# A decoder layer on one core: scans and three fillers in the routing of the experts, and a last norm without waits on stores

## The reference

```python
x = _layernorm(x + _L0_attn_ref(x, Wq, Wkv, q_g, q_b, k_g, k_b, Wwin, bwin, Wout))
x = _layernorm(x + _L0_xattn_ref(x, ctx_1024, ctx_1024))
x = _layernorm(x + _L0_ffn_ref(x, router_w, expert_w1, expert_w2))
# _L0_ffn_ref:
scores = xf @ router_w.T
top_v, top_i = jax.lax.top_k(scores, TOP_K)
routing_w = jax.nn.softmax(top_v, axis=-1)
for e in range(NUM_EXPERTS):
    w_e = jnp.sum(jnp.where(top_i == e, routing_w, 0.0), axis=-1)
    h = jax.nn.gelu(xf @ expert_w1[e].T, approximate=False)
    out = out + h @ expert_w2[e].T * w_e[:, None]
```

## Time and profile before

| | us |
|---|---|
| median of 3 runs | 1164.17 (1163.9 to 1164.26) |
| the profiled execution | 1166.83 |
| its span | 1164.9 |
| from the last `attend` to the first fetch of rows | 643 to 687.7 |
| the experts | 688 to 1129.4 |
| the last norm | 1129.4 to 1164.9 |

### The profile page before, as it was taken

One profiled execution on the slowest core, in us unless ns is written; L12 is line 12 of the kernel. 1 busy time (PEld: TensorE's weight loads), 2 busy tenths in 40 slices (PEclk: granted clock), 3 DMA queues, 4 the chain that ended last, 5 costly groups with the idle time before them and its releaser, 6 DMA issues.

```text
span 1164.9 us, 24917 instructions
## 1 busy us (share of the span) xinstructions
PE 948.5 (81%) x8069; PEld 762.1 (65%) x8070; DVE 813.1 (70%) x1196; ACT 481.8 (41%) x1132; POOL 712.0 (61%) x461
## 2 busy tenths in 40 slices
PE   7984079998999989768878249999999999999940
PEld 4542079897888888746656237777777777777730
DVE  4899999999999998248888764444444444444435
ACT  3676334444555554436656223223333223333315
POOL 3576499999999999300000055666666667666522
PEclk9998589999999999979999569999999999999985
DMA  3262102221121212477674412222222222222236
GB/s 103 64 129 35 45 19 69 68 68 57 56 68 68 67 46 67 164 261 270 203 249 163 168 29 38 44 43 45 45 45 41 45 45 43 44 44 43 30 91 220
DMA packets 69916, 100.24 MB, mean 86 GB/s; under 512 B 9248, under 2 KB 51680, under 8 KB 68928
## 3 DMA queue, kind: packets, MB, share of 16 engines
q1 hardware_dynamic: 52816, 76.85, 21.1%
q0 software_dynamic: 15904, 18.66, 10.1%
q10 hardware_dynamic: 1152, 4.19, 0.9%
HBM read 73.82 MB, written 26.25 MB: 86 GB/s over the span
## 4 chain that ended last, share of the span: by engine, by line
PE 45%; issue 17%; POOL 17%; DVE 11%; DMA 5%; ACT 4%; SPq 0%; POOLq 0%; DVEq 0%; ACTq 0%
PE psum L760 16%; PE psum L768 10%; POOL mid L1191 9%; PE psum L770 5%; PE psum L619 3%; DMA sum_dram<-arena,mid 2%; PE psum L599 2%; PE psum L662 2%; POOL arena L1196 2%; POOL arena L1182 1%; PE psum L752 1%; POOL arena L1202 1%; DVE arena L1579 1%; PE psum L688 1%; PE psum L602 1%
## 5 line engine op out<-in xcount | busy, mean ns | idle before, releaser
L619 PE MATMUL psum<-consts,mid 128*128 128x128 f32 x2176 | 252.8, 278 | 52.1 <-POOL mid L1191 52.1
L760 PE MATMUL psum<-arena 128*128 128x128 f16 x3408 | 286.5, 220 | 4.1 <-issue 2.6
L760 PEld LDWEIGHTS psum<-arena 128*128 x3408 | 239.2, 98 | 75.3 <-issue 9.6
L619 PEld LDWEIGHTS psum<-consts,mid 128*128 128x128 f32 x2176 | 247.9, 193 | 61.8 <-issue 48.4
L1191 POOL TENSOR_TENSOR mid<-arena 128x2304 f32<-128x2304 f32 (+1 forms) x62 | 251.3, 4075 | 9.6 <-POOL arena L1182 7.6
L768 PE MATMUL psum<-arena 128*128 x568 | 215.1, 380 | 4.9 <-DVE arena L1736 1.2
L1269 POOL DMA_INDIRECT sum_dram<-arena,mid x71 | 141.4, 1991 | 43.4 <-issue 20.5
L1745 DVE SCALAR_TENSOR_TENSOR arena<-psum,arena 128x256 f32<-128x256 f32 x71 | 34.4, 484 | 186.2 <-ACT arena L1088 120.1
L1430 DVE TENSOR_REDUCE arena<-mid 128x272 f32<-128x4624 f32 x32 | 158.9, 4967 | 1.7 <-ACT mid L894 1.2
L1088 ACT ACTIVATE arena<-psum,arena 128x256 f32<-128x256 f32 x71 | 33.7, 475 | 296.4 <-PE psum L770 296.4
L770 PE MATMUL psum<-arena 128*128 x568 | 154.8, 273 | 0.0
(11 more groups left out here) (196 smaller groups left out, 1443.8 us busy)
## 6 DMA issues: line engine op xcount, KB each, us to landing
arena<-w_t SPq DMA_DIRECT2D x64, 256.0 KB, 2.8
arena<-w_t SPq DMA_DIRECT2D x16, 1024.0 KB, 10.5
arena<-x SPq DMA_DIRECT2D x32, 128.0 KB, 2.1
arena<-x_dram SPq DMA_DIRECT2D x8, 512.0 KB, 5.0
arena<-ctx_t SPq DMA_DIRECT2D x8, 512.0 KB, 5.8
arena<-ctx SPq DMA_DIRECT2D x8, 512.0 KB, 6.5
x_dram<-mid SPq DMA_DIRECT2D x8, 512.0 KB, 3.3
arena<-sum_dram SPq DMA_DIRECT2D x8, 512.0 KB, 5.0
```

The source lines that it names most:

```text
L619: last = nc.tensor.matmul(psum[:, u, c * P:(c + 1) * P], products[half][:, w, c * P:(c + 1) * P], ident, start=(a + w == 0 and c == 0), st ...
L760: last = nc.tensor.matmul(dst, block_of(w, e, 0, c * F + j * P, P), x[:, u, c * P:(c + 1) * P], start=(k == 0 and c == 0), stop=(k == 2 an ...
```

## The change

- **End of the cross attention.** The last sequence's `norm2` no longer has a `low_part` in front. TensorE transposes x2 tile by tile, each as soon as it is normed, into four banks; ScalarE copies each tile for itself, and the router's products follow tile by tile. The eight last weight parts are dealt out anew: `low_part(6, 1, 1)` and `low_part(7, 0, 0)` stand ahead of `copy_logits`, `low_part(7, 0, 1)` in the wait for the two counting products, and `low_part(7, 1, 0)` and `(7, 1, 1)` behind `routed`.
- **Three fillers.** `keep_running(n)` multiplies the identity by itself n times into an unused bank: 8 times ahead of the last `norm2`, 10 behind the router's products, 12 behind the transpose of the gates.
- **Scans.** `picked`, `upto` and `place` lie expert by expert, and one scan instruction sums the tile counts over all 256 columns; the sum goes on from one expert to the next, and `ends` takes what came before off. A second scan sums the lots. The constants under the diagonal are less by one, so `place` needs one addition fewer. The sum over the eight experts writes whole numbers itself, and the comparisons read them as they are.
- **Sources first.** `slot_src` is made ahead of the mark of empty slots, and GpSimd fetches rows on `sources_made`.
- **Last norm.** `sum3` lies in the space of the weights and has a place for each of the eight groups, so no load and no norm waits for a store. The moments are four aggregation instructions (`bn_aggr`) and one addition. GpSimd norms the fourth row of each group, ScalarE three, all in place.

```diff
+            def keep_running(n):
+                for _ in range(n):
+                    nc.tensor.matmul(psum[:, 5, 0:P], ident, ident, start=True, stop=True)
             pe.wait_ge(sum2_done, T // P)
-            transpose_x2(B - 1, 1)
-            route(B - 1)
-            pe.wait_ge(picked_made, 1)
+            keep_running(8)
+            for t in range(QT):
+                pe.wait_ge(normed2, QT * (B - 1) + t + 1)
+                for c in range(C):
+                    last = nc.tensor.transpose(psum[:, t, c * P:(c + 1) * P], x1_n[:, 1, t, c * P:(c + 1) * P], ident)
+                last.then_inc(tile_turned, 1)
+            for t in range(QT):
+                pe.wait_ge(tile_copied, t + 1)
...
+            keep_running(10)
+            pe.wait_ge(gap_and_picks, 2)
...
+            keep_running(12)
+            pe.wait_ge(routed, 2)
             pe.wait_ge(w_low_made, 4 * N_EXP)
...
-            high_parts(N_EXP - 1, 0)
+            for t in range(QT):
+                act.wait_ge(tile_turned, t + 1)
+                nc.scalar.activation(x2_t[:, :, t * P:(t + 1) * P], psum[:, t, 0:C * P].rearrange("p (c n) -> p c n", n=P),
+                                     ACT.Copy).then_inc(tile_copied, 1)
+            high_part(N_EXP - 1, 0, 0)
             keep_x2(B - 1, 1)
-            x2_transposed(B - 1)
+            high_part(N_EXP - 1, 0, 1)
+            nc.scalar.activation(count_psum, consts[:, AT_COUNT:AT_COUNT + P], ACT.Copy).then_inc(count_and_gap, 1)
+            act.wait_ge(gap_and_picks, 1)
+            nc.scalar.activation(top_v[:, 1, :], top_v[:, 1, :], ACT.Exp).then_inc(count_and_gap, 1)
             high_parts(N_EXP - 1, 1)
...
-            def norm3(g, u, v):
-                if g >= 2:
-                    act.wait_ge(out_stored[u], 16 * (g // 2))
+            def norm3(g):
                 act.wait_ge(shift3_made, g + 1)
-                for t in range(QT):
+                for t in range(QT - 1):
+                    nc.scalar.activation(sum3[:, g, t, :], sum3[:, g, t, :], ACT.Identity, bias=bias3[:, g, t:t + 1],
+                                         scale=rstd3[:, g, t:t + 1]).then_inc(out_ready, 1)
...
-            pool.wait_ge(routed, 1)
+            pool.wait_ge(sources_made, 1)
...
+            for g in range(GROUPS3):
+                root(rstd3[:, g, :], QT, B + g + 1)
+                pool.wait_ge(rstd_ready, B + g + 1)
+                t = QT - 1
+                nc.gpsimd.tensor_scalar(sum3[:, g, t, :], sum3[:, g, t, :], mean3[:, g, t:t + 1], rstd3[:, g, t:t + 1],
+                                        ALU.subtract, ALU.mult).then_inc(last_ready, 1)
...
-                if past(b, 1):
-                    low_part(b - 1, 1, 1)
+                if more:
+                    if past(b, 1):
+                        low_part(b - 1, 1, 1)
...
-            for k in range(2):
-                for half in range(2):
-                    low_part(N_EXP - 1, k, half)
+            low_part(N_EXP - 2, 1, 1)
+            low_part(N_EXP - 1, 0, 0)
             copy_logits(B - 1, 1)
...
-            while hop < TILES:
-                nc.vector.tensor_copy(upto[1 - at][:, 0:hop, :], upto[at][:, 0:hop, :])
-                n_scan += 1
-                done(nc.vector.tensor_tensor(upto[1 - at][:, hop:, :], upto[at][:, hop:, :], upto[at][:, 0:TILES - hop, :],
-                                             ALU.add), scan_step, n_scan)
-                at, hop = 1 - at, 2 * hop
+            done(nc.vector.tensor_tensor_scan(upto.rearrange(flat), psum[:, 1, 0:TILES * N_EXP], picked.rearrange(flat), 0.0,
+                                              ALU.add, ALU.max), scan_step, 2)
+            nc.vector.tensor_copy(ends[:, 1:], upto[:, :, TILES - 1]).then_inc(scan_step, 1)
+            nc.vector.tensor_tensor(place.rearrange(flat), upto.rearrange(flat), psum[:, 0, 0:TILES * N_EXP],
+                                    ALU.add).then_inc(place_made, 1)
...
+            slot_done(nc.vector.tensor_scalar(slot_pair, slot_f[:, 1, :], -1.0, None, ALU.add))
+            nc.vector.tensor_scalar(slot_src, slot_pair, T - 1, None, ALU.bitwise_and).then_inc(sources_made, 1)
...
+            low_part(N_EXP - 1, 1, 0)
+            low_part(N_EXP - 1, 1, 1)
...
-                moments(stats3[:, u], mean3[:, v, :], rstd3[:, v, :], g)
+                for t in range(QT):
+                    nc.vector.bn_aggr(norm3_of[:, g, t, :], stats3[:, g, t, :]).then_inc(moments3_made, 1)
+                dve.wait_ge(moments3_made, QT * (g + 1))
+                nc.vector.tensor_scalar(rstd3[:, g, :], rstd3[:, g, :], EPS, None, ALU.add).then_inc(var_made, 1)
```

More of the change, by code:

```diff
@@ L47 @@
 TILES = T // P
+GROUPS3 = TILES // QT
 MASKED = 1e10
@@ L84, in host_consts @@
         i + 1.0,
-        T + i * 1.0,
     ]
@@ L210, in decoder_layer @@
         chosen = next_low("route", TOP, TILES, N_EXP)
-        picked = next_low("route", TILES, N_EXP)
-        upto = [next_low("route", TILES, N_EXP) for _ in range(2)]
-        place = next_low("route", TILES, N_EXP)
+        picked = next_low("route", N_EXP, TILES)
+        upto = next_low("route", N_EXP, TILES)
+        place = next_low("route", N_EXP, TILES)
         placed = next_low("route", TOP, TILES, N_EXP)
@@ L216, in decoder_layer @@
         low_used["route"] = TOP * TILES * P // 2
-        lots = next_low("route", 2, N_EXP)
+        ends = next_low("route", N_EXP + 1)
+        lots_end = next_low("route", N_EXP)
         lots_n = next_low("route", N_EXP)
@@ L1277, in _ @@
                     fetch_gates(s - 4, s % 4)
-            for g in range(TILES // QT):
-                root(rstd3[:, g % 4, :], QT, B + g + 1)
+            for g in range(GROUPS3):
+                root(rstd3[:, g, :], QT, B + g + 1)
[3 more added lines that the diff above has]
+                                        ALU.subtract, ALU.mult).then_inc(last_ready, 1)
         @block.vector
@@ L1647, in _ @@
-            now, hop = 0, 1
-            while hop < N_EXP:
-                nc.vector.tensor_copy(lots[:, 1 - now, 0:hop], lots[:, now, 0:hop])
-                lots_done(nc.vector.tensor_tensor(lots[:, 1 - now, hop:], lots[:, now, hop:], lots[:, now, 0:N_EXP - hop], ALU.add))
-                now, hop = 1 - now, 2 * hop
-            lots_end = lots[:, now, :]
-            done(nc.vector.tensor_tensor(place, upto[at], tile_count, ALU.subtract), place_made, 1)
-            done(nc.vector.tensor_tensor(place, place, psum[:, 0, 0:TILES * N_EXP].rearrange("p (t n) -> p t n", n=N_EXP),
-                                         ALU.add), place_made, 2)
@@ L1669, in _ @@
-            done(nc.vector.tensor_copy(spot_row, spot_i[:, 0].rearrange(flat)), spot_back, 2)
+            lots_done(nc.vector.tensor_tensor_scan(lots_end, lots_n, lots_n, 0.0, ALU.add, ALU.max))
+            lots_done(nc.vector.tensor_tensor(lots_n, lots_end, lots_n, ALU.subtract))
+            lots_done(nc.vector.scalar_tensor_tensor(lots_n, lots_n, float(P), ends[:, 0:N_EXP], ALU.mult, ALU.subtract))
+            dve.wait_ge(place_made, 1)
+            done(nc.vector.tensor_tensor(place, place, lots_n.unsqueeze(2).to_broadcast([P, N_EXP, TILES]), ALU.add), place_made, 2)
@@ new lines, in _ @@
+            by_tile = place.rearrange("p n t -> p t n").unsqueeze(1).to_broadcast([P, TOP, TILES, N_EXP])
+            done(nc.vector.tensor_tensor(placed, chosen, by_tile, ALU.mult), spot_step, 2)
+            with nc.allow_low_precision(reason="one of the eight is a whole number, the others are zero"):
+                found = nc.vector.tensor_reduce(spot_i[:, 0], placed, op=ALU.add, axis=AX.X)
+            done(found, spot_step, 3)
+            done(nc.vector.tensor_scalar(spot_i[:, 1], spot_i[:, 0], P.bit_length() - 1, None, ALU.logical_shift_right), spot_step, 4)
```

161 lines of the change are left out of this document (64 added, 97 removed).

## The result

| | before | after |
|---|---|---|
| median of the runs, us | 1164.04 (1162.39 to 1164.26) | 1151.24 (1150.18 to 1152.72, 4 runs) |
| the profiled execution, us | 1166.83 | 1152.72 |
| its span, us | 1164.9 | 1150.9 |

The ratio is 0.9894, with a 95% interval of 0.9877 to 0.9911: 12.8 us faster, where 19.6 were forecast. 1151.24 lies above the range of 1141.5 to 1150. From profile to profile the span fell by 14.0 us; that is more than 12.8, because the profiled executions lie 2.8 (before) and 1.5 (after) above their medians.

The account below looks back on a forecast made before the run. Bound by small dependent VectorE instructions in the routing and by group-after-group work in the last norm. Gains 5.0 + 4.2 + 0.85 + 0.4 + 9.1 = 19.55 us bring 1164.17 to 1144.6 us; range 1141.5 to 1150.

Parts of the forecast that it names:

- the last norm: From the last sum's landing to the end: ScalarE leads at 2.04 us a group, no group waits for stores; gain 9.1.
- the dear end: Last norm, GpSimd's root of 1.01 plus a row sized at 0.735 us: together 1.9 us, under ScalarE's 2.04.
- the transfers or GpSimd: Rival: mixed transfers (4 us more) or a 1.3 us GpSimd row (2.5 later) lead the last norm; 1147 to 1148.6, chance 0.2.
- from the copy of the logits to the scan: Routing stretch after the router: fillers keep the clock, `low_part(7,0,1)` fills VectorE's wait, scan starts at 653.7; 0.9 us gained.
- which is less than the 3.0: Second filler's end to `picked`: a 2.3 us gap, shorter than the 3.0 after which the clock fell, so clock kept.
- the scans: Routing, from the scan to the first `is_slot`: 4.6 us instead of 8.84, scan taken as 0.69; gain 4.2.
- They hide by 0.3 us: Two `low_part` behind `sources_made` end at 689.5, before the first fetched rows land at 689.9, so they cost nothing.
- The copy of the logits: End of the attention: copy starts at 649.3 instead of 653.43, set by VectorE at 2.4 GHz; 4.1 us earlier.
- The sources: Before the first fetch: three of seven VectorE instructions move behind `sources_made`; gain 0.85 us.
- that rival: Rival: GpSimd's first fetch is held by the two `low_part` beside it, 0.98 us once or twice; 1145.6 to 1146.6, chance 0.1.
- The fetch-to-landing term: Start of the expert loop: third filler raises the clock, the forty-eight products take 4.1 us instead of 4.37; gain 0.4.
- The clock is not kept: Rival: identity products fail to hold the clock in the routing's first waits; 2.9 us lost, 1147.5, chance 0.15.

Follow-up runs that it names:

- run 2: Kernel after plus one tiny fill on GpSimd that waits until every store has landed; 1158.27 us in one execution.
- run 7: Kernel after, but GpSimd norms the fourth row only in groups 0, 2, 4 and 6, ScalarE in the odd groups; 1147.47 us, ratio 0.9868.
- run 1: Kernel after with the fourth row of each group normed by ScalarE again, GpSimd doing only the last norm's roots; 1151.57 us, ratio 0.9877.
- run 3: Kernel after without the third filler, the twelve identity products behind the gates' transpose; 1151.57 us, ratio 0.9887.
- run 6: Kernel after, but GpSimd's row uses two numbers in the instruction instead of mean and root from memory; 1147.94 us in one execution.
- run 4: Kernel after with fourteen identity products behind the router's instead of ten; 1153.57 us, ratio 0.9901.
- run 5: Kernel before with only the new last norm; routing, weight split and sources as before, some signals sharing a semaphore; 1160.3 us, ratio 0.9967.
- run 8: Kernel after without any of the three fillers (8, 10 and 12 identity products); 1152.65 us, ratio 0.9904.
- run 9: Kernel after with GpSimd's rows in even groups alone, 14 products in the second filler and no third filler; 1149.07 us, ratio 0.9874.

## Why the prediction was wrong, step by step

**Wrong, the last norm: 9.1 us forecast, 4.1 measured.** Two steps of the sum failed.

The first is the term "its nearest row is two inputs of 256 columns, 0.735 us, together 1.9 at the dear end, under 2.04". The row took 1.23. That was called the dear end, though the nearest row had another form: one operation on two tiles instead of two operations on one. With a root of 1.03 and a row of 1.23 GpSimd leads at 2.33 a group, where the working had ScalarE lead at 2.04. The last store was issued 24.8 us behind the landing instead of 22.6: 2.1 us. The rival had this mechanism at nearly this price ("If GpSimd's row took 1.3 us, its period is 2.4 and the end 2.5 later"), at a chance of 0.2 shared with the transfers.

The second failed step isn't in the working at all: the end was taken as the issue of the last store plus the 3.4 us that lay behind it before, and 0.4 for the transfers, 3.8 in all. But 6.7 us lay behind it: the store landed in 2.7, and GpSimd's drain ended 3.7 later. Runs 2 and 7 show that the drain sets the end, run 1 that the store does once the drain is out of the way. 2.1 and 2.9 make the 5.0 us that were missed. The two work together: a row on GpSimd costs twice, since it slows the groups and also stands last in front of the drain.

**Wrong in size, from the copy of the logits to the scan: 0.9 forecast, -0.06 measured.** The step "which is less than the 3.0" gave the clock as kept. The gap was 2.48 us, less than the 3.0 too, and yet the counting products ran at 0.54 and took 1.96 us, where they take 1.13 at 2.4 GHz. A fall seen once, at 3.0, was no bound. So it was in the profiles of after and of run 1; in those of runs 2, 3, 6 and 7, with the same ten products, the way from copy to scan was 4.48, near the 4.4 of the working, but there because the clock had fallen earlier and was back in time. The Trainium skill, page "TensorE: Matmul & The Clock Gate", section "Part 1: The HAM clock gate (the "warmup" mystery)", ties the clock to how busy the array has been of late. The traces agree in so far as the gap of 1.60 behind 14 fast products (run 4) left it up and the gap of 2.48 did not; the falls while TensorE was busy (run 3, 0.59) they leave unexplained.

**Slightly off, the scans: 4.2 forecast, 3.88 measured.** The scan took 0.69 us, as the row of 512 columns that it was sized by, which agrees with the half throughput that the prediction quotes from the Trainium skill, page "DVE: opcode table, instruction layouts, handler registers and perf-mode slots", section "Datapath and trigger behaviour". The other terms of the sum add up to 3.91, not 3.93, which changes nothing. The 0.3 come from the product over 512 columns, 1.03 instead of 0.69: its input `by_tile` now reads `place` across its order. The layout that serves the scan is paid for there.

**Wrong, and hidden by the spread: "They hide by 0.3 us".** The two `low_part` beside the first fetch end 2.86 us after its start and the rows land at 3.0 to 3.1, as expected. But the first transposes come at 3.85 to 4.21 in all nine profiles with the two there, against 3.03 and 3.09 in the two without them (before, run 5). In run 7 even the third filler is over by then, so it isn't that. Timeline of run 7, and two lines of its chain of work:

```profile
674.39 2.84 PE L714 MATMUL psum<-consts 128*128 128x128 f32 x24
...
675.57 2.67 DVE L1584 SCALAR_TENSOR_TENSOR arena<-arena,mid 128x1024 f16<-128x1024 f32 x2
...
679.23 0.93 PE L758 MATMUL psum<-consts,arena 128*128 128x128 f32 x4 [2.00 <-DMA arena<-x_dram,mid]
```

```profile
675.38 3.08 DMA arena<-x_dram,mid
678.46 0.78 issue
```

Where no slow filler stands in the way (runs 3, 4 and 6 to 9), the transposes start 1.0 to 1.2 us behind the end of the second `low_part`. In the code TensorE waits for all low parts first and only then reads the word that names the experts of its lots (`load_word`), so that stretch probably holds this read; no run moved the wait, so the cause is not shown. What the 0.8 us are worth to the end can't be told either: the third lot's products start 15.36 and 14.02 after the fetch in the two kernels without the `low_part`, and 14.7 to 16.3 in the others.

**Right.** The root alone, 1.01. The copy of the logits, 4.10 for 4.1, set by VectorE; and in run 8, at 1.2 GHz, later by 0.29 where "half a microsecond" stood. The sources, 0.82 for 0.85. The first fetch isn't held by `low_part`: 1.24 us against 1.22, so that rival is out. The expert loop kept its phase.

**Luck.** The fetch-to-landing term, 0.5 for 0.4: the third filler ran at 1.2 GHz throughout (5.33 us), the transposes came 4.21 after the fetch instead of 3.03, the first 48 products took 4.45 us instead of 4.1, run 3 shows no gain of the filler, and run 5, with the loop and the routing of before, took 439.6 from fetch to landing where before took 441.7. A gain of half a microsecond can't be seen beside that.

**The rivals.** "The clock is not kept" was half true and cheaper than priced: 0.83 of the 2.9, and the slow ten, taken there to end after `picked`, end 0.9 us ahead of it. In "the transfers or GpSimd" it was GpSimd; no wait for a transfer grew. "Slower than before" didn't happen.

**Open.** Why the clock fell in runs 2, 3, 6, 7 and 9 while TensorE was busy isn't settled; in runs 2, 3, 6 and 7 nothing ahead of the counting products was edited, so the same instructions gave both. What lengthens the loop by up to 4.6 us from profile to profile isn't settled either. And what GpSimd does in the 7 us of its drain no trace shows, only that they follow its last work.

## What to carry to other kernels

Ask of each engine what the program's end waits for after that engine's last instruction, not only when the last result lands: two ends that fall together in the profile look like one, and the hidden one takes over as soon as the other moves. Don't size an instruction by a row of the same columns but another form, and where its engine's new period comes within 10% of the one that leads (1.9 against 2.04), price the case that it leads. Before work is given to an idle-looking engine, see whether that engine's last instruction is on the path: half the rows on GpSimd (28.6 us from landing to end) were better than all (31.4) and than none (29.5). And don't take a fall of the clock that was seen once for the shortest there is.

## What the runs showed of the hardware

- GpSimd's DRAIN at the end of the program lasts until 6.9 to 7.0 us behind its last work in all eleven profiles, after a root, a row or a fill of 0.12 us. VectorE's took 0.20 us, ScalarE's 0.15. The Trainium skill, page "VectorE: DVE Perf Modes", section "The DRAIN you can't avoid", speaks of drains of about 12 ns at a program's beginning and end on all engines; SyncE's had 13 ns here, and GpSimd's, ScalarE's and VectorE's didn't follow.
- One input with two operations on GpSimd, 128x256 in f32, took 1.23 us with values per partition and 1.075 with numbers, against 0.735 for a product of two inputs. The Trainium skill, page "GPSIMD Engine Reference", section "3.1 Elementwise — side-by-side cycle accounting", has two inputs as the dearer case; here the form with one input was the slower, though it also has a second operation, and no run tells the two apart.
- A scan of 256 columns on VectorE, one input in PSUM, took 0.69 us, a copy of as many 0.42, and a product of 512 columns 0.69 in order and 1.03 with one input across its order.
- Multiplying the identity doesn't hold the granted clock for certain: in run 3 it fell to a mean of 0.59 in a window in which TensorE was busy throughout with the router's products and the identity's, and so it went in five of the eight profiles that have ten or 14 of them behind the router.
